# g turned by transposing DMAs, odd y high halves on ScalarE, statistics spread over the chunk

## The reference, cut to what matters

```python
xn = layernorm(x)                       # x: 4 x 2048 x 512 f32
q, k, v = xn @ Wq.T, xn @ Wk.T, xn @ Wv.T          # each 4 x 2048 x 128
# for each time step t:  r_t = q_t @ M.T ;  M = 0.99 * M + v_t.T @ k_t / 4
s = (r @ Wo.T) * sigmoid(gate)
h = layernorm(xn) * gamma + beta        # 8192 rows x 512
y = silu(h @ dequant(fc1_q) + b1)       # 512 -> 2048
z = y @ dequant(fc2_q) + b2             # 2048 -> 512
out = x + s * silu(xn + 0.5 * z)
```

## Time and profile before

| | |
|---|---|
| median of 3 runs | 1283.18 us (1282.25 to 1283.63) |
| profiled execution, own time | 1284.9 us |
| its span, first to last instruction | 1283.1 us |
| mean granted TensorE clock | 0.98 of full |
| PE, DVE, ACT, POOL busy | 93%, 89%, 71%, 62% of the span |

### The profile page before, as it was taken

One profiled execution on the slowest core, in us unless ns is written; L12 is line 12 of the kernel. 1 busy time (PEld: TensorE's weight loads), 2 busy tenths in 40 slices (PEclk: granted clock), 3 DMA queues, 4 the chain that ended last, 5 costly groups with the idle time before them and its releaser, 6 DMA issues.

```text
span 1283.1 us, 18950 instructions
## 1 busy us (share of the span) xinstructions
PE 1196.5 (93%) x6028; PEld 620.7 (48%) x6028; DVE 1144.5 (89%) x1966; ACT 904.8 (71%) x1574; POOL 798.6 (62%) x778
## 2 busy tenths in 40 slices
PE   2778999999999999999999999999999999999993
PEld 1344455555545555554555555455555545555540
DVE  8678999999899999989999998999999899998986
ACT  6556767777776767777676777767677776767771
POOL 4068865947576594757659475765947576594614
PEclk9789999999999999999999999999999999999997
DMA  9511040211204021120402112040211203020111
GB/s 331 172 38 33 1 99 1 67 34 37 63 1 99 1 66 34 36 65 1 100 1 67 34 33 66 1 100 1 66 34 36 64 2 99 1 66 1 33 35 33
DMA packets 41621, 65.69 MB, mean 51 GB/s; under 512 B 11696, under 2 KB 11952, under 8 KB 41008
## 3 DMA queue, kind: packets, MB, share of 16 engines
q1 hardware_dynamic: 41232, 64.36, 18.9%
q10 hardware_dynamic: 288, 0.08, 0.0%
HBM read 47.59 MB, written 16.81 MB: 50 GB/s over the span
## 4 chain that ended last, share of the span: by engine, by line
PE 74%; DVE 12%; ACT 7%; issue 6%; DMA 1%; POOL 0%; SPq 0%; ACTq 0%; DVEq 0%; POOLq 0%
PE blk L479 27%; PE blk L497 25%; PE side L439 7%; DVE blk L750 5%; PE side L464 4%; PE side L428 3%; ACT blk L623 3%; PE side L456 2%; DVE y_split L741 2%; ACT z_rows L638 1%; DVE y_split L736 1%; PE side L415 1%; PE side L458 1%; PE side L457 1%; PE side L449 1%
## 5 line engine op out<-in xcount | busy, mean ns | idle before, releaser
L750 DVE TENSOR_TENSOR blk<-blk,ratio_rows 128x512 f32<-128x512 f32 x960 | 643.2, 688 | 88.4 <-PE blk L497 86.5
L623 ACT ACTIVATE blk<-blk,ratio 128x512 f32<-128x512 f32 x768 | 508.0, 665 | 255.7 <-PE blk L479 250.0
L479 PE MATMUL blk<-h_split,q_sb 128*128 128x512 f16 x2048 | 614.4, 382 | 13.8 <-issue 8.1
L497 PE MATMUL blk<-w_sb,y_split 128*128 128x512 f16 x2048 | 610.7, 380 | 1.2 <-DVE blk L750 1.2
L497 PEld LDWEIGHTS blk<-w_sb,y_split 128*128 128x128 f16 x2048 | 200.0, 98 | 247.2 <-DVE blk L750 6.5
L479 PEld LDWEIGHTS blk<-h_split,q_sb 128*128 128x128 f16 x2048 | 196.2, 98 | 224.6 <-issue 39.9
L630 ACT ACTIVATE y_full<-blk,par,last 128x512 f32<-128x512 f32 x256 | 201.3, 786 | 85.0 <-PE blk L479 84.5
L741 DVE SCALAR_TENSOR_TENSOR y_split<-y_full,up,y_split 128x512 f16<-128x512 f32 x256 | 219.6, 858 | 0.1
L1045 POOL CAST h_split<-h_full 128x512 f16<-128x512 f32 x64 | 52.8, 826 | 239.9 <-ACT h_full L579 239.9
L736 DVE TENSOR_SCALAR y_split<-y_full,up 128x512 f16<-128x512 f32 x256 | 170.0, 664 | 0.0
L1033 POOL TENSOR_SCALAR g_rows<-xt,mv,gs 128x512 f32<-128x512 f32 x60 | 133.4, 2232 | 0.0
(11 more groups left out here) (150 smaller groups left out, 1081.7 us busy)
## 6 DMA issues: line engine op xcount, KB each, us to landing
xt<-in_x SPq DMA_DIRECT2D x64, 256.0 KB, 4.7
x_again<-in_x SPq DMA_DIRECT2D x256, 64.0 KB, 1.9
out<-z_rows SPq DMA_DIRECT2D x256, 64.0 KB, 1.7
w_sb<-in_q SPq DMA_DIRECT2D x4, 1024.0 KB, 14.0
ratio_rows<-ratio_dram SPq DMA_DIRECT2D x4, 1024.0 KB, 9.1
y_split<-in_q SPq DMA_DIRECT2D x1, 1024.0 KB, 10.3
h_split<-in_q SPq DMA_DIRECT2D x1, 1024.0 KB, 12.6
z_rows<-in_q SPq DMA_DIRECT2D x1, 1024.0 KB, 14.5
```

Source lines behind the costliest of these rows:

```text
L479: mm = pe.matmul(blk[J % 2][:], q1_sb[:, g, j // 4, w, j % 4 * P:(j % 4 + 1) * P], a[:, c % 2, g, :], start=(g == 0 and n == 0), stop=(g = ...
L497: mm = pe.matmul(blk2[:, i, :], y[:, J % Y_RING, rows], w2_sb[:, j, part, :], start=(j == 0 and n == 0), stop=(j == FB - 1 and n == len(te ...
L623: act.activation(blk[J % 2][:], blk[J % 2][:], ACT.Copy, scale=ratio1[:, at:at + 1]).then_inc(blk_scaled, 1)
L750: dve.tensor_tensor(blk2[:, i, :], blk2[:, i, :], ratio2_rows[:, j, :], ALU.mult).then_inc(blk2_scaled, 1)
```

## The change

- The four `turn` jobs leave PE. ACT now writes the f16 high half of each g tile from SBUF (`g_high`, slots 38 to 41), POOL the low half (`g_low`, queue slots 39 to 45), both into `g_split`, and SP turns each half with a transposing DMA (`turn_g`, eight per chunk, 128x512 f16) into `g_hi` and `g_lo`.
- h is then made from the turned halves: ACT `h_part` from `g_hi` (slots 51, 53, 55, 57), DVE `h_sum` adds gamma times `g_lo` (52 to 58), POOL splits it as before (53 to 59). `h_part` waits for all eight transposes and for its buffer of the ring of two.
- `normalise` is a multiply and an add with a prepared shift in place of a subtract and a multiply, in place in `xt` (slots 36 to 39); `rows` has two more small steps and sits in slot 31.
- The high half of y of odd blocks goes from DVE to ACT (`odd_y_high`).
- `stats` of the next chunk are in slots 2, 10, 18, 26, `moments` in 27 and 28.

```diff
-STATS_AT, MOMENTS_AT = (0, 1, 2, 3), (5, 6)
+STATS_AT, MOMENTS_AT = (2, 10, 18, 26), (27, 28)
-NORMALISE_AT = (36, 38, 40, 42)
-PREPARE_AT, ROWS_AT, FIRST_ROWS_AT = (0, 3, 15, 18), 7, 28
+NORMALISE_AT = (36, 37, 38, 39)
+PREPARE_AT, ROWS_AT, FIRST_ROWS_AT = (0, 3, 15, 18), 31, 31
-TURN_AT = (51, 54, 56, 59)
+G_HIGH_AT, G_LOW_AT = (38, 39, 40, 41), (39, 41, 43, 45)
+H_PART_AT, H_SUM_AT, H_SPLIT_AT = (51, 53, 55, 57), (52, 54, 56, 58), (53, 55, 57, 59)
...
+            def turn_g(c):
+                sp.wait_ge(h_done, 4 * c)
+                sp.wait_ge(kv_done, 4 * c)
+                sp.wait_ge(q_done, c)
+                for i in range(NT):
+                    sp.wait_ge(g_lo_rows, NT * (c - 1) + i + 1)
+                    for n, to in enumerate((g_hi, g_lo)):
+                        sp.dma_start_transpose(to[:, :, i * P:(i + 1) * P], g_split[:, n, i, :]).then_inc(g_turned, 16)
...
-                    pe.wait_ge(g_lo_done, 4 * c + 4)
+                        pe.wait_ge(g_turned, 2 * NT * 16 * c)
...
+            def g_high(c, i):
+                act.wait_ge(g_done, NT * c + i + 1)
+                wait(act, g_turned, 2 * NT * 16 * (c - 1))
+                act.activation(g_split[:, 0, i, :], g_rows[:, i, :], ACT.Copy).then_inc(g_hi_rows, 1)
+            def h_part(c, k):
+                act.wait_ge(g_turned, 2 * NT * 16 * c)
+                act.wait_ge(h_done, 4 * c + k - 1)
+                act.activation(h_full[:, k % 2, :], g_hi[:, k, :], ACT.Identity,
+                               bias=beta_s[:, k:k + 1], scale=gamma_s[:, k:k + 1]).then_inc(h_part_done, 1)
...
+            def odd_y_high(J):
...
+                act.activation(y_hi[:, J % Y_RING, :], y_full[:, J % 2, :], ACT.Copy, scale=up_y
+                               ).then_inc(y_hi_odd_done, 1)
...
+            def h_sum(c, k):
+                dve.wait_ge(h_part_done, 4 * (c - 1) + k + 1)
+                dve.scalar_tensor_tensor(h_full[:, k % 2, :], g_lo[:, k, :], gamma_s[:, k:k + 1], h_full[:, k % 2, :],
+                                         ALU.mult, ALU.add).then_inc(h_full_done, 1)
...
-                pool.tensor_scalar(g_rows[:, i, :], xt[:, i, :], mv[:, c % 2, i, 0:1],
-                                   gs[:, c % 2, i:i + 1], ALU.subtract, ALU.mult).then_inc(g_done, 1)
+                pool.tensor_scalar(g_rows[:, i, :], xt[:, i, :], gs[:, c % 2, i:i + 1],
+                                   g_shift[:, c % 2, i:i + 1], ALU.mult, ALU.add).then_inc(g_done, 1)
+            def g_low(c, i):
+                pool.wait_ge(g_hi_rows, NT * (c - 1) + i + 1)
+                pool.tensor_tensor(g_split[:, 1, i, :], g_rows[:, i, :], g_split[:, 0, i, :], ALU.subtract
+                                   ).then_inc(g_lo_rows, 1)
```

More of the change, by code:

```diff
@@ L20 @@
 TOP = 2.0 ** 14
-ROW_STEPS = 10
+ROW_STEPS = 12
 TINY = 1e-30
@@ L85, in side_job @@
             return None
-        job, i = SIDE[e]
-        c += 1 if job == "turn" else 0
-        return (job, c, i) if c < NCH and not (job == "turn" and c == 0) else None
+        return (SIDE[e][0], c, SIDE[e][1]) if c < NCH else None
     def job_behind(G, lag, kind):
@@ L98, in finishing, with next_chunk @@
         return (c - 1, at.index(e)) if c > 0 and e in at else None
+    def next_chunk(G, at):
+        c, e = divmod(G, STEPS)
+        return (c + 1, at.index(e)) if c < NCH - 1 and e in at else None
     def fc1_step(G):
@@ L197, in build @@
         x_again = sb("x_again", [P, NT, H], F32)
-        g_rows = sb("g_rows", [P, NT, H], F32)
+        g_rows = xt
+        g_split = sb("g_split", [P, 2, NT, H], F16)
         s_rows = sb("s_rows", [P, S_RING, H], F32)
@@ L383, in _ @@
                         load_again(c, i)
+                if c < NCH - 1:
+                    turn_g(c + 1)
             for n in range(NT):
@@ L406, in bank_free @@
                     pe.wait_ge(s_out, n)
[L407 to L416, removed]
             def run_side(G):
@@ L421, in run_side @@
                 bank_free(G)
-                if job == "turn":
-                    turn(c, i, bank)
-                elif job == "q":
+                if job == "q":
                     for k in range(KC):
@@ L431, in run_side @@
                 elif job == "kv":
-                    if i == 0:
-                        pe.wait_ge(g_lo_done, 4 * c + 4)
+                    if i == 0 and c == 0:
+                        pe.wait_ge(g_lo_done, 4)
+                    elif i == 0:
+                        pe.wait_ge(g_turned, 2 * NT * 16 * c)
                     if c == 0 and i == 0:
@@ L564, in _, with first_g_high, first_h @@
                            zero_c[:].unsqueeze(1).to_broadcast([P, FB, T]), ACT.Copy).then_inc(q1_low_zero, 1)
[L566 to L578, removed]
+            def first_g_high(k, bank):
+                act.wait_ge(turn_done, k + 1)
+                act.activation(g_hi[:, k, :], bank[:], ACT.Copy).then_inc(first_g_hi_done, 1)
+            def first_h(k, bank):
+                act.wait_ge(h_scales, 1)
+                act.wait_ge(turn_done, k + 1)
+                wait(act, h_done, k - 1)
                 act.activation(h_full[:, k % 2, :], bank[:], ACT.Identity,
                                bias=beta_s[:, k:k + 1], scale=gamma_s[:, k:k + 1]).then_inc(h_full_done, 1)
+            def g_high(c, i):
[7 more added lines that the diff above has]
+                               bias=beta_s[:, k:k + 1], scale=gamma_s[:, k:k + 1]).then_inc(h_part_done, 1)
             def q_copy(c, i, bank):
@@ L631, in silu @@
                                scale=last1[:, j:j + 1]).then_inc(silu_done, 1)
+            def odd_y_high(J):
+                wait(act, blk2_done, NT * (J - Y_RING + 1))
+                if J == 1:
+                    act.wait_ge(y_scale, 1)
+                act.wait_ge(silu_done, J + 1)
+                act.activation(y_hi[:, J % Y_RING, :], y_full[:, J % 2, :], ACT.Copy, scale=up_y
+                               ).then_inc(y_hi_odd_done, 1)
             def gate_silu(c, i):
@@ L658, in _ @@
             for k in range(KC):
-                h_whole(0, k, first_turn_bank[k])
-                g_high(0, k, first_turn_bank[k])
+                first_h(k, first_turn_bank[k])
+                first_g_high(k, first_turn_bank[k])
             act.wait_ge(wqkv_scale, 1)
@@ L677, in _ @@
                         silu(at[0])
+                if (at := fc1_step(G - YHIGH_LAG) if G >= YHIGH_LAG else None) and at[1] == KC - 1 and at[0] % 2:
+                    odd_y_high(at[0])
                 if G in Q1_AT:
@@ L691, in _ @@
                     s_copy(*at, side[JOB_BANK[G - S_LAG]])
[L692 to L695, removed]
+                if at := next_chunk(G, G_HIGH_AT):
+                    g_high(*at)
+                if at := next_chunk(G, H_PART_AT):
+                    h_part(*at)
                 if at := finishing(G, GATE_AT):
@@ L713, in first_normalise, with first_g_low @@
                                   gs[:, 0, i:i + 1], ALU.subtract, ALU.mult).then_inc(g_done, 1)
[L715 to L719, removed]
+            def first_g_low(k, bank):
+                dve.wait_ge(h_full_done, k + 1)
+                dve.wait_ge(first_g_hi_done, k + 1)
                 dve.tensor_tensor(g_lo[:, k, :], bank[:], g_hi[:, k, :], ALU.subtract).then_inc(g_lo_done, 1)
+            def h_sum(c, k):
+                dve.wait_ge(h_part_done, 4 * (c - 1) + k + 1)
+                dve.scalar_tensor_tensor(h_full[:, k % 2, :], g_lo[:, k, :], gamma_s[:, k:k + 1], h_full[:, k % 2, :],
+                                         ALU.mult, ALU.add).then_inc(h_full_done, 1)
             def mask_scores(c, i, bank):
@@ L739, in y_low @@
             def y_low(J):
-                dve.wait_ge(y_hi_done, J + 1)
+                if J % 2:
+                    dve.wait_ge(y_hi_odd_done, J // 2 + 1)
+                else:
+                    dve.wait_ge(y_hi_done, J // 2 + 1)
                 dve.scalar_tensor_tensor(y_lo[:, J % Y_RING, :], y_full[:, J % 2, :], up_y, y_hi[:, J % Y_RING, :],
@@ L897, in _ @@
             top_of_q1(3).then_inc(tops_made, 1)
-            g_low(0, 0, first_turn_bank[0])
+            first_g_low(0, first_turn_bank[0])
             pick(OF_Q1)
-            g_low(0, 1, first_turn_bank[1])
+            first_g_low(1, first_turn_bank[1])
             largest(OF_Q1, top_q1[:])
@@ L911, in _ @@
                               ALU.mult, ALU.mult).then_inc(s1_scaled, 1)
-            g_low(0, 2, first_turn_bank[2])
-            g_low(0, 3, first_turn_bank[3])
+            first_g_low(2, first_turn_bank[2])
+            first_g_low(3, first_turn_bank[3])
             dve.wait_ge(wqkv_hi_done, 1)
@@ L948, in _ @@
                     mask_scores(*at, side[JOB_BANK[G - MASK_LAG]])
-                if at := job_behind(G, GLOW_LAG, "turn"):
-                    g_low(*at, side[JOB_BANK[G - GLOW_LAG]])
+                if at := next_chunk(G, H_SUM_AT):
+                    h_sum(*at)
```

(14 more changed lines are left out.)

23 lines of the change are left out of this document (11 added, 12 removed).

## The result

The changed kernel takes 1320.63 us (median of 4 runs, 1318.96 to 1321.84) against 1283.41 before: ratio 1.028, 95% interval 1.027 to 1.030, so 37 us slower. The forecast was 1292. The sign was right, the size a quarter. The profiled execution took 1318.96 us.

A forecast was written before the change was run, and what follows sets the result against it. The prediction took PE to bound the kernel, needing 72.3 of 74.88 us a chunk. Its terms, -1.75 - 0.7 + 0.4 + 1.9 + 0.7, gave +0.55 us a chunk, +8 us over 15 chunks, hence 1292 us, range 1260 to 1335.

The forecast's parts named there:

- PE is the bound and its need falls by 1.75 us: PE needs 72.3 of a 74.88 us chunk; removing the four turns takes off 1.75 us, all of it counting.
- The transposing DMAs: SP's eight transposes before slot 51: at 0.97 us each, no cost; at 1.5 us each, +3.7 us a chunk.
- The threshold of that step: SP's issue interval up to 1.04 us costs nothing before h_part(0); beyond, each 0.1 us costs ACT 0.8 us.
- transposes late: Rival: SP's interval above 1.04 us; 1347 us at 1.5, 1324 at 1.31; chance 0.22 together with normalise slow.
- rows, normalise, g_high: +1.9: POOL's rows and normalise delay ACT's g_high and rescales, so PE's slot 44 starts late: +1.9 us a chunk, bounds 0.8 and 2.8.
- y rows on ACT: +0.4: Odd y high halves on ACT, landing beside gate_silu in slots 20 and 28: +0.4 us a chunk, bounds 0 and 1.2.
- DVE's waits: -0.7: Waits for DVE in slots 11 to 35 shrink as y rows leave: -0.7 us a chunk, bounds 0 and 1.84.
- h from turned halves: +0.7: Slots 51 to 63: h_part waits for the ring of two, delaying PE's slot 60: +0.7 us a chunk, bounds 0 and 2.
- The sum: All terms of a middle chunk together: +0.55 us a chunk, +8 us over 15 chunks.

The follow-up runs named there:

- Experiment 2: The change with hi and lo of a tile turned by one transposing DMA of 128x1024, 4 a chunk in place of 8: 1291.98 us, ratio 1.007.
- experiment 1: The change with statistics in slots 0 to 3, moments 5 and 6, rows 7, normalise queued on POOL in 31 to 34: 1281.7 us.
- Experiment 8: The kernel of experiment 6 with g_high in slots 35 to 38 and h_part in 48, 51, 54, 57: 1265.27 us, ratio 0.986.
- experiment 3: The change with odd_y_high removed, so all y high halves stay on DVE: 1308.63 us, ratio 1.020.
- experiment 6: The change with rows early, one transposing DMA a tile, and only y high halves of blocks 1, 3, 7, 9 on ACT: 1300.74 us, ratio 1.014.
- Experiment 9: The kernel of Experiment 8 with y high halves of blocks 5 and 15 also back on ACT, six blocks: 1252.32 us, ratio 0.975.
- experiment 10: The kernel before the change with y high halves of blocks 1, 3, 5, 7, 9 on ACT: 1271.53 us, ratio 0.990.

## Why the prediction was right and wrong, point by point

- **PE is the bound and its need falls by 1.75 us**: held. 70.5 us (72.3 with the turns) plus the sum of the table's waits gives the period of every kernel within 0.2 us.
- **The transposing DMAs: this step failed.** It put them at nothing, "no cost, by a hair", with SP's interval at 0.97 us, the middle of two bounds far apart. The interval measured 1.31 us (1.27 and 0.04 between), and the last one landed 2.5 us after its issue began, where 1.9 was taken from plain copies. Experiment 2, which takes away four of the eight issues and nothing else, gives 29 of the 37 us back; experiment 1, which starts them earlier, ends at 1282.
- **The threshold of that step was off too.** A landing counts from the start of its own issue, so seven intervals lie ahead of the eighth and not eight: (645.2 - 1.9 - 635.0) / 7 = 1.19 us, not 1.04. With eight intervals of 1.31 the prediction's formula gives a wait of 2.2 us. With seven, the longer landing and the first transpose 53.6 us into the chunk (54.2 by the prediction), it gives 53.6 + 7 x 1.31 + 2.5 = 65.3; ACT was ready for h_part(0) at 64.3 (64.4 by the prediction), so 1.0 us. The trace has 0.94 of idle ACT there, and PE's slot 53 is 1.05 above that of experiments 1 and 2, in chunks 2 to 5; in chunks 6 to 14 PE's wait is 0.9 us longer still.
- **The rival "transposes late" is what happened**, and the sign that was named for it, a wait of h_part that a DMA ends, is in the trace. It was put at 1347 us for 1.5 us and at 1324 for 1.31. That 1324 lies so near 1320.63 is luck: it has 2.2 us a chunk from the formula with eight intervals, and the trace has 1.05 in the first chunks and more later by something that the rival doesn't name. The Trainium skill's 1309 ns ("VectorE: DVE Perf Modes", The three transpose paths) is for a block of 128x128; here 128x512 took about that to issue, and 128x1024 too, so the number was near and the scaling by blocks would have been wrong.
- **rows, normalise, g_high: +1.9**: held in place and size. Slots 40 to 43 have 1.73. Rows ended 48.6 us into the chunk (49.0 said), and experiment 1 shows what of it is waiting for POOL (0.9) and what is the packing of four copies between rescales (0.8).
- **y rows on ACT: +0.4 was too low**: 0.99 (slots 6, 30, 31), inside its bound of 1.2. I had looked at slots 16 to 22, which took it without a wait, and overlooked slot 4.
- **DVE's waits: -0.7 was too low**: 1.63 went. The statistics in slots 10 and 18 did no harm.
- **h from turned halves: +0.7 was too low**: slots 54 to 59 have 1.34 and slot 53 has 0.71 without any DMA wait, 2.05 in all and 1.33 more than before, inside its bound of 2. Experiment 8 takes 1.2 of it away with a step of three slots.
- **The sum.** With the measured terms for chunks 2 to 5: -1.75 - 1.63 + 0.99 + 1.73 + 1.33 + 1.05 = +1.72, and the period rose by 1.74. Without the transposes it is +0.67, where +0.55 was said: that part came out by errors of 0.6, 0.6 and -0.9 that cancel, which is luck, as is that experiment 2 measures the forecast of 1292. Over the span, 14 chunks (1 to 14) times 1.74 are 24 us, the nine later ones have 1.4 us more each, 13 us, and chunk 0 and the end are 3 us shorter: 34 us, which is what the span grew by. For the later chunks' 1.4 us the prediction had no term.

**What the errors leave open: slot 35.** It waits 1.28 us in experiments 3, 6 and 8 and only 0.41 before, with the y row of slot 28 (block 5) on DVE in all. Experiment 9 empties it together with slot 11 (blocks 5 and 15 on ACT), experiment 10 empties it alone (block 5), so block 5's rows are what DVE is late by. DVE's and POOL's timelines show where the time goes. Before, POOL was idle from 617.92 to 619.60, and both rows of block 5 started in that gap:

```profile
618.39 0.48 DVE L736 TENSOR_SCALAR y_split<-y_full,up 128x512 f16<-128x512 f32 x1
619.38 0.74 DVE L741 SCALAR_TENSOR_TENSOR y_split<-y_full,up,y_split 128x512 f16<-128x512 f32 x1
```

In experiment 6 both start while POOL works on an output:

```profile
626.22 1.27 POOL L1145 TENSOR_TENSOR z_rows<-z_rows,x_again 128x512 f32<-128x512 f32 x1
626.90 0.87 DVE L771 TENSOR_SCALAR y_split<-y_full,up 128x512 f16<-128x512 f32 x1
628.11 1.27 POOL L1142 TENSOR_TENSOR z_rows<-z_rows,s_rows 128x512 f32<-128x512 f32 x1 [0.62 <-ACT z_rows L667]
628.29 1.63 DVE L779 SCALAR_TENSOR_TENSOR y_split<-y_full,up,y_split 128x512 f16<-128x512 f32 x1
```

They take 1.28 us more, the next y low row takes 0.43 less, and the wait is 0.87 longer. In the whole trace of before, 243 of the 244 y rows that started with POOL idle are within 10% of the shortest (0.47 us for a high row, 0.73 for a low one); of the 268 that started beside a POOL operation 141 are longer than that, up to 1.52 us. So a POOL operation is beside nearly every long y row. That it is the cause is inferred from these rows; no run isolates it, nor shows why POOL's outputs moved against DVE's rows.

## What to carry to other kernels

A transfer with no row in the trace is a term whose middle value hides a threshold: work out the value at which it starts to cost, and if both bounds lie on either side of it, forecast the two cases and not the middle. When many DMAs are issued behind each other ahead of one wait, the issue time of the instruction is the price, so put more into each. Whether a row can be moved to another engine is decided slot by slot: four y rows moved gave 14 us, all eight cost 2. The price of a row is to be read in its own slot, not as a mean: in the trace of before a y high row took 0.47 to 1.58 us, and nearly all the long ones stood beside work of POOL.

## What the runs showed that I had not expected

**The clock falls after the longer wait.** In chunks 1 to 6 of the changed kernel TensorE's granted clock is full all through. Seven of the eight chunks from 7 to 14 have 3.4 us at the lower level right behind the wait of slot 53. PE's timeline and the stretches (PEclk is the column behind the busy times):

```profile
657.28 0.93 PE L485 MATMUL blk<-h_split,q_sb 128*128 128x512 f16 x2 [2.34 <-ACT blk L636]
658.00 1.06 PE L503 MATMUL blk<-w_sb,y_split 128*128 128x512 f16 x2
658.85 1.06 PE L485 MATMUL blk<-h_split,q_sb 128*128 128x512 f16 x2
659.71 1.06 PE L503 MATMUL blk<-w_sb,y_split 128*128 128x512 f16 x2
```

```profile
655.00:658.00 3.00, 0.72 (x3) 0.27 (x3) 1.29 (x3) 2.14 (x4) 0.47 (x1) 0.90 0.83 198
658.00:661.00 3.00, 3.00 (x9) 1.11 (x8) 2.27 (x5) 2.85 (x5) 2.14 (x3) 0.53 0.86 171
661.00:664.00 3.00, 3.00 (x16) 1.29 (x14) 3.00 (x5) 2.80 (x5) 1.32 (x3) 1.00 0.00 0
```

PE had been idle for 2.34 us; the pairs behind it start 0.86 us apart in place of 0.43, at 1.2 GHz and not 2.4. In experiments 1, 2 and 9, with 0.7 us in that slot, the clock of the middle chunks is never below full. So a wait that PE sees can be paid twice. The second price is 0.5 to 0.8 us a chunk: chunk 13, idle for 2.20 us and with no fall of the clock, is 0.6 us longer than the early ones, just by its longer wait, and chunk 11, idle for 2.37 with a fall, is 1.4 longer, 0.8 of it by the wait. The length of the wait alone doesn't decide: chunk 6 was idle for 2.43 us with no fall, and experiment 3 has 2.16 with none and 2.39 with one. What else decides isn't shown.

**Some transposes issue in 2.0 to 2.2 us** where most take 1.27: none in chunks 1 to 5, and one each in seven of the nine chunks from 6 to 14, adding 0.6 to 0.9 us to the wait (1.2 in chunk 9, where an issue also began late). The other two, chunks 10 and 14, have eight issues of the common length and a late landing: in chunk 10 the last transpose landed 4.08 us after its issue began in place of 2.50. Together these make the later chunks' longer wait. The first experiment has them too (one of 2.23 us in the shown chunk), and they cost it nothing, since the last transpose there lands before it is wanted. What makes the slow issues and the late landings isn't shown.
